# Expert halves of a mixture layer as one float32 product each, clipped straight from PSUM, with the order of all pieces drawn up anew

## What is computed

```python
h = _L0_tok_ref(x, ...)                       # gated recurrence; 257 positions come out
h = h + _L0_attn_ref(_layernorm(h), ...)      # 8 heads; k and v from a sequence of the other half of the batch
h = h + _L0_ffn_ref(_layernorm(h), ...)       # mixture of 16 experts, best 2, and a shared one

def swiglu5(h, alpha, gate_scale, up_shift, gate_clamp_raw, up_clamp_raw):
    g = jnp.clip(h[..., ::2], -gate_clamp, gate_clamp)
    u = jnp.clip(h[..., 1::2], -up_clamp, up_clamp)
    return g * jax.nn.sigmoid(g * alpha) * gate_scale * (u + up_shift)
# every expert on every position, then the weighted sum:
he = jnp.einsum('nd,edh->enh', xf, expert_w1) + expert_b1[:, None, :]
te = swiglu5(he, ...)
oe = jnp.einsum('enh,ehd->end', te, expert_w2) + expert_b2[:, None, :]
y = jnp.einsum('ne,end->nd', cw, oe)
```

## Time and profile before

| | us |
|---|---|
| median of 3 runs | 441.05 |
| lowest and highest run | 439.95 and 443.12 |
| span of the profiled execution, first to last instruction | 434.7 |
| PE, DVE busy | 334.7, 322.2 |
| ACT, POOL busy | 243.9, 157.3 |

### The profile page before, as it was taken

One profiled execution on the slowest core, in us unless ns is written; L12 is line 12 of the kernel. 1 busy time (PEld: TensorE's weight loads), 2 busy tenths in 40 slices (PEclk: granted clock), 3 DMA queues, 4 the chain that ended last, 5 costly groups with the idle time before them and its releaser, 6 DMA issues.

```text
span 434.7 us, 6229 instructions
## 1 busy us (share of the span) xinstructions
PE 334.7 (77%) x2160; PEld 269.7 (62%) x2160; DVE 322.2 (74%) x500; ACT 243.9 (56%) x412; POOL 157.3 (36%) x125
## 2 busy tenths in 40 slices
PE   4028089875787998997869998987799997778863
PEld 1015068554477685884658676967677786667752
DVE  7894577235488779696798599696884599697991
ACT  2647425543466755863666566834584685475541
POOL 1000751010054585341346466330242165163761
PEclk9658558987976999996987999998899999698995
DMA  7302900006600000029000000065000000000000
GB/s 283 155 0 99 169 1 2 2 0 171 98 0 2 0 2 2 0 99 147 24 0 0 0 0 0 0 178 90 2 0 2 2 0 2 19 8 0 1 2 24
DMA packets 12407, 17.21 MB, mean 40 GB/s; under 512 B 984, under 2 KB 9184, under 8 KB 12256
## 3 DMA queue, kind: packets, MB, share of 16 engines
q1 hardware_dynamic: 12384, 16.91, 15.9%
HBM read 11.63 MB, written 5.28 MB: 39 GB/s over the span
## 4 chain that ended last, share of the span: by engine, by line
PE 38%; DVE 36%; issue 8%; DMA 8%; ACT 4%; SPq 4%; POOL 1%; POOLq 0%; DVEq 0%; ACTq 0%
PE slot L956 37%; DVE tbuf L881 6%; DVE gbuf L869 5%; DMA ks<-spill 4%; DVE ubuf L875 4%; DVE mx L783 4%; DVE rden L798 2%; SPq L409 2%; DMA spill<-qhl 2%; DVE ubuf L891 2%; SPq L403 1%; DVE rmax L712 1%; DMA cst<-in_consts 1%; DVE zs L733 1%; DVE h2n L802 1%
## 5 line engine op out<-in xcount | busy, mean ns | idle before, releaser
L498 POOL TENSOR_TENSOR te<-tbuf,ubuf 128x516 f32<-128x516 f32 x52 | 71.6, 1378 | 70.1 <-DVE tbuf L881 52.5
L956 PE MATMUL slot<-xh,w1h 128*128 128x258 f32 x208 | 67.8, 326 | 6.9 <-DVE ubuf L891 5.0
L956 PE MATMUL slot<-te,w 128*128 128x258 f32 x208 | 53.8, 406 | 13.6 <-POOL te L498 13.6
L956 PE MATMUL slot<-xl,w1h 128*128 128x258 f32 x208 | 61.8, 297 | 0.0
L956 PE MATMUL slot<-xh,w1l 128*128 128x258 f32 x208 | 61.8, 297 | 0.0
L488 POOL TENSOR_TENSOR ubuf<-ubuf,cwb 128x516 f32<-128x516 f32 x24 | 33.7, 1403 | 76.6 <-ACT cwb L660 76.1
L956 PEld LDWEIGHTS slot<-te,w 128*128 128x128 f32 x208 | 40.0, 199 | 24.3 <-POOL te L498 18.0
L869 DVE TENSOR_SCALAR gbuf<-gbuf,fpar 128x516 f32<-128x516 f32 x52 | 48.0, 923 | 5.7 <-ACT gbuf L640 5.6
L783 DVE TENSOR_REDUCE mx<-slot 128x2 f32<-128x514 f32 x64 | 41.8, 686 | 13.0 <-PE slot L956 12.9
L956 PEld LDWEIGHTS slot<-xh,w1h 128*128 128x128 f32 x208 | 42.6, 205 | 12.2 <-DVE ubuf L891 5.6
L640 ACT ACTIVATE gbuf<-slot,cst 128x516 f32<-128x516 f32 x52 | 36.1, 694 | 19.9 <-PE slot L956 18.4
(11 more groups left out here) (161 smaller groups left out, 643.2 us busy)
## 6 DMA issues: line engine op xcount, KB each, us to landing
qs<-spill SPq DMA_DIRECT2D x12, 258.0 KB, 4.4
ks<-spill SPq DMA_DIRECT2D x24, 129.0 KB, 5.8
spill<-qhl SPq DMA_DIRECT2D x4, 516.0 KB, 2.9
spill<-khl SPq DMA_DIRECT2D x4, 516.0 KB, 3.6
...
te<-in_sel SPq DMA_DIRECT2D x1, 832.0 KB, 11.1
```

The costliest lines, as they stand in the source:

```text
L498: g.tensor_tensor(te[:, c % NTE, :, :], tbuf[:, c % NB, :, :], ubuf[:, c % NB, :, :], ALU.mult)\
L956: return nc.tensor.matmul(out_, lhsT, rhs, start=start, stop=stop, **k)
```

## The change

A half becomes one float32 product of the weights by the input, two instructions in the program (one per sequence) in place of six. The bias moves into the weights: the features of the normalised input sum to zero, so feature 0's weight row can be subtracted from all rows, which frees that row for the bias (and, for the up half, bias plus shift), with the input's feature 0 set to one. `copy` (ACT, an affine copy with a scale and a bias per partition) makes that input in place of the split by ACT and DVE. The clips of DVE now read PSUM and write gbuf and ubuf, and release the slot; the two copies by ACT per chunk are gone. Once, at the start, DVE subtracts the row and adds the shift in place of the split of the weights, and SP loads one more array of 1664 KB and a row of 6.5 KB. All of `TIMES` is new.

```diff
     "FAT": {
-        "chunk": {"g": 0.0, "clip_up_1": 0.29, "u": 0.44, "gated_1": 0.69, "cw_1": 0.67, "clip_gate": 0.47},
+        "chunk": {"g": 0.017, "clip_gate": 0.019, "u": 0.575, "clip_up": 0.622, "gated_1": 0.664, "cw_1": 0.681},
...
-            sp.dma_start(w1_stage, w1_in).then_inc(s_w1, 16)
+            sp.dma_start(w1[:, :, :, :].rearrange("p k c n -> p (k c n)"), w1_in).then_inc(s_w1, 16)
+            sp.dma_start(w0_stage, w0_in).then_inc(s_w1, 16)
+            sp.dma_start(shift_stage, shift_in).then_inc(s_w1, 16)
...
-                        act.wait_ge(s_w1, 16)
-                        a(w1h[:, :, :, :].rearrange("p k c n -> p (k c n)"), w1_stage, ACT.Copy).then_inc(s_high, 1)
...
-                a(xh[:, :, :], xn2[:, :, :], ACT.Copy).then_inc(S["xh"], 1)
+                first = const("first")
+                a(xf[:, :, :], xn2[:, :, :], ACT.Identity, bias=first[:, 1:2], scale=first[:, 0:1]).then_inc(S["xf"], 1)
...
-            def gate_half(st, u, c):
-                filled(act, st, ("g", c))
-                if c >= NB:
-                    ge(act, "gg", NF * u + c + 1 - NB)
-                release(a(gbuf[:, c % NB, :, :], slot(st, ("g", c))[:, :, 0:W], ACT.Identity, bias=par[:, B1G, c:c + 1]),
-                        st, ("g", c))
...
-            def tanh(u, c):
-                ge(act, "gclip", NF * u + c + 1)
+            def clip_gate(st, u, c):
+                released(act, st, ("g", c))
...
-            def split(st, u):
-                ge(dve, "xh", u + 1)
-                v.tensor_tensor(xl[:, :, :], xn2[:, :, :], xh[:, :, :].bitcast(F32), ALU.subtract).then_inc(S["xl"], 1)
-
             def clip_gate(st, u, c):
-                released(dve, st, ("g", c))
-                p = c % NB
-                v.tensor_scalar(gbuf[:, p, :, :], gbuf[:, p, :, :], fpar[:, GHI, c:c + 1], fpar[:, GLO, c:c + 1],
-                                ALU.min, ALU.max).then_inc(S["gclip"], 1)
+                name = ("g", c)
+                filled(dve, st, name)
+                ge(dve, "gg", NF * u + max(0, c + 1 - NB))
+                release(v.tensor_scalar(gbuf[:, c % NB, :, :], slot(st, name)[:, :, 0:W], fpar[:, GHI, c:c + 1],
+                                        fpar[:, GLO, c:c + 1], ALU.min, ALU.max), st, name)
...
-            def low_weights():
-                dve.wait_ge(s_high, 1)
-                then(v.tensor_tensor(w1l[:, :, :, :].rearrange("p k c n -> p (k c n)"), w1_stage,
-                                     w1h[:, :, :, :].rearrange("p k c n -> p (k c n)").bitcast(F32), ALU.subtract))
+            def fold_inputs():
+
+                dve.wait_ge(s_w1, 48)
+                then(v.tensor_tensor(w1[:, :, :, :].rearrange("p k c n -> p (k c n)"),
+                                     w1[:, :, :, :].rearrange("p k c n -> p (k c n)"), w0_stage, ALU.subtract))
+                up_bias = w1[0:1, 1, :, :].rearrange("p c n -> p (c n)")
+                then(v.tensor_tensor(up_bias, up_bias, shift_stage, ALU.add))
...
                 for s in range(2):
-                    o = slot(st, name)[:, s, 0:W]
-                    mm(o, w1h[:, k, c, :], xh[:, s, :], stop=False)
-                    mm(o, w1h[:, k, c, :], xl[:, s, :], start=False, stop=False)
-                    last = mm(o, w1l[:, k, c, :], xh[:, s, :], start=False)
+                    last = mm(slot(st, name)[:, s, 0:W], w1[:, k, c, :], xf[:, s, :])
                 fill(last, st, name)
```

More of the change, by code:

```diff
@@ L74 @@
     "FAT": {
-        "chunk": {"g": 0.0, "clip_up_1": 0.29, "u": 0.44, "gated_1": 0.69, "cw_1": 0.67, "clip_gate": 0.47},
[L76 to L85, removed]
+        "chunk": {"g": 0.017, "clip_gate": 0.019, "u": 0.575, "clip_up": 0.622, "gated_1": 0.664, "cw_1": 0.681},
+        "down": (5.755, 10.144, 13.709),
+        "add": (5.969, 10.326, 14.276),
+        "out": 20.644,
@@ L86 @@
+        "project": {"center": 9.925, "variance": 10.709, "scale": 11.145, "project": 11.934},
     },
     "FA": {
[L88 to L93, removed]
@@ L94 @@
-        "norm": {"center": 9.1, "variance": 10.05, "scale": 11.38, "gate": 12.1},
-        "route": (12.68, 13.66, 14.06, 14.17, 14.45),
-        "late": {"split": 15.0, "cwt": 15.1, "keep": 16.01},
+        "chunk": {"g": -0.288, "clip_gate": -0.079, "u": 0.519, "clip_up": 0.7, "gated_1": 0.051, "cw_1": 0.7},
+        "down": (6.268, 10.406, 14.138),
+        "add": (6.278, 10.413, 16.432),
+        "out": 16.957,
+        "attend": ({"begin": -0.048, "max": 0.332, "mlast": 0.2, "mtop": 0.328, "plast": 0.336, "st": 0.337, "pv": 0.0, "norm": 0.627},
+                   {"begin": 2.144, "max": 0.398, "mlast": 0.267, "mtop": 0.3, "plast": 0.294, "st": 0.136, "pv": 0.202, "norm": 2.922}),
@@ L97 @@
+        "norm": {"center": 9.134, "variance": 10.641, "scale": 11.221, "gate": 11.982},
+        "route": (12.68, 13.007, 14.04, 14.17, 15.568),
+        "late": {"copy": 13.182, "cwt": 14.662, "keep": 14.752},
     },
     "F": {
-        "chunk": {"g": 0.0, "clip_up_1": 0.11, "u": 0.4, "gated_1": 0.69, "cw_1": 0.7, "clip_gate": 0.47},
-        "down": (5.69, 10.26, 13.85),
-        "add": (6.22, 10.25, 14.63),
-        "out": 17.19,
+        "chunk": {"g": -0.497, "clip_gate": -0.223, "u": -0.25, "clip_up": -0.156, "gated_1": 0.478, "cw_1": -0.027},
@@ L103 @@
+        "down": (6.297, 10.413, 15.749),
+        "add": (6.569, 10.209, 15.785),
+        "out": 16.331,
     },
     "AT": {
-        "attend": ({"begin": -0.09, "max": 0.2, "mlast": 0.21, "mtop": 0.5, "plast": 0.33, "st": 0.36, "pv": 0.15, "norm": 0.2},
-                   {"begin": 1.65, "max": 0.4, "mlast": 0.37, "mtop": 0.33, "plast": 0.4, "st": 0.22, "pv": 0.2, "norm": 0.43}),
-        "norm": {"center": 9.1, "variance": 10.05, "scale": 11.1, "gate": 12.02},
-        "route": (12.16, 13.23, 13.66, 14.06, 14.07),
@@ L209, in use, with build @@
         return n % NSLOT, before
-def build(nc, x_in, consts_in, sel_in, w1_in, w2_in, spill, out):
+def build(nc, x_in, consts_in, sel_in, w1_in, w0_in, shift_in, w2_in, spill, out):
     ctx = ExitStack()
```

94 lines of the change are left out of this document (49 added, 45 removed).

## The result

The changed kernel takes 447.44 us (446.27 to 452.37, 4 runs) against 440.50 us (439.69 to 443.12, 4 runs) for the kernel before beside it: ratio 1.021 (95% interval 1.015 to 1.027). It is slower, by 1.5 to 2.7%.

A forecast was written before the change was run, and what follows sets the result against it. It took PE and DVE, neither full, to be bound by waiting for each other in a circle each step. Terms -1.2 - 1.8 + 0 - 4.5 = -7.5 us gave span 427.2, plus 6.35: 433.5 us, range 421 to 446.

The forecast's parts named there:

- Loop, two steps: Both loop steps: -1.9 us from h1 to q, +1.0 us from first maximum to h2n, each step; -1.8 us together.
- Rival 1: First maximum to h2n, three steps: PE waits more, at lower clock; +9.0 us a step, 446 to 457 us; chance 0.17.
- Rival 2: Whole kernel: DVE was the bound, its contention vanishes (-15 us) and PE's clock rises; 424 to 427 us; chance 0.22.
- Rival 3: Whole kernel: no difference, PE's +13.5 us eat DVE's 15 us; 440 us; chance 0.20.
- One half: PE, each of 104 halves: 0.90 us for 0.77, 0.13 us dearer, adding 13.5 us at full clock.
- One clip: DVE, each clip out of PSUM: 0.69 us, taken from L891, bounds 0.55 and 1.5; DVE busy 15 us less.
- First and second step: Before the loop: nothing in the first step; q's transfer starts earlier in the second, -1.2 us.
- h2n to the spill: Loop, h1 to q: four dearer halves replace six and the gate; -1.9 us a step.
- Spill to the next maximum: Loop, the way through memory: transfers unchanged, rest of F still the later end in the first step; 0 us.
- Step without T: Up to h2n +1.0 us, then -1.0 us with PE coming out ahead of DVE; 0 us in sum.
- Last step: Last step: DVE's clips shorten and PE becomes the bound; -4.5 us, to 53 to 54 us.
- The time: Whole kernel: span 427.2 us plus 6.35 us between span and median time gives 433.5 us.

The follow-up runs named there:

- att_direct: Kernel before with clips out of PSUM, releasing the slot, for chunks 0 to 8 in both loop steps and throughout the last step; 447.9 us, ratio 1.024.
- c_old: Kernel before with all clips reading PSUM, each right behind its product, ACT's copies gone, biases left out, three float32r products kept; 454.1 us, ratio 1.032.
- p_only: Kernel before with one float32 product a half in place of three float32r, order and ACT's copies kept; 446.2 us, ratio 1.014.
- co: Changed kernel's table and PSUM clips, but with the three float32r products of the kernel before, biases left out; 449.0 us.
- hold_old: Kernel before, ACT's copies and SBUF clips kept, but DVE's clip releases the slot and stands right behind its product; 480.0 us.
- pos_only: Kernel before with each clip placed right behind its product, ACT's copy still releasing the slot (control for hold_old); 461.9 us, ratio 1.048.
- f_clip: Kernel before with clips out of PSUM in the last step only, right behind their products, old order, bias folded into weights; 431.1 us, ratio 0.984.
- pc_old: Changed kernel with the table of the kernel before, each clip right behind the product it reads; 460.4 us, ratio 1.047.
- fa_direct: Kernel before with PSUM clips in the last step, in the changed order, and for chunks 9 to 12 of the step without T; 434.5 us, ratio 0.988.

## Why the prediction was wrong

- **The step that failed** is in "Loop, two steps": +1.0 us a step from the first maximum to h2n. It let PE's 4.0 us of extra work vanish into PE's 8.6 us of idle time but for 2.1 us, and gave DVE a gain of 1.1. Measured: PE's work grew by 4.1 and 7.4 us, its idle time did not shrink but grew by 3.5 and 0.8, and the stretches by 7.6 and 7.8 us. "A slot is now released by DVE in its own order, and PE waits for DVE where ACT had freed it" stood under ACT and had no price. In before's table, with no work added, clips that read PSUM cost +6.3 and +5.7 us in att_direct and +7.1 and +5.7 in c_old, while the product alone costs these stretches nothing (p_only). In after the table changed too, so its +7.6 and +7.8 us are not split: co, with the old product, has +10.4 and +8.1.
- **Rival 1** had the place and the size ("a loss once those stretches grow by more than 3.5 us each", 446 us in its mild form), but not the mechanism: the clock in the stretch is 0.92 and 0.90, on the whole no lower than before's 0.88 and 0.91. Of its sum the 2 us of waits were the right part (PE idles 3.5 and 0.8 us more). Rival 2's clock did rise a little (0.870 to 0.892 over the span), and its 15 us of DVE did not come. Rival 3's balance was not what happened.
- **One half.** 0.88 us to the next float32 product, 0.90 forecast, and 0.15 us more a half than three float32r products where PE is full, 0.13 forecast. PE's total came out at 347.9 us. In the old table the product costs 6 us, in the new one none that can be told (co).
- **One clip.** 0.80 us, not 0.69, so L891 was no measure of it: 104 x 0.11 = 11.4 us. `gated` went from 0.900 to 0.956 us, 2.9 us more. That is the 14 us by which DVE missed. The clip never stretches, as forecast. The Trainium skill ("VectorE: DVE Perf Modes", the errata table) has 120 cycles and one per element for a read of PSUM, by which a clip of 516 would be an estimated 0.66 us; the traces say 0.80. The same page of the Trainium skill (Rules for kernel authors) offers a choice between reading PSUM and copying out first by the number of operations; in hold_old against pos_only, who frees the slot weighs 18.1 us with the same operations.
- **First and second step.** -1.7 us for -1.2; but from the first maximum to unit 1's spill nothing was won (44.6 to 44.4 us), so the q forecast was wrong and the rest lies in the start, which varies by more among the runs (first maximum of all at 54.4 to 62.5 us).
- **h2n to the spill.** -1.7 us a step, -1.9 forecast: right.
- **Spill to the next maximum.** +1.5 and +3.1 us where nothing was forecast. In the second loop step the transfer, 5.75 us in the earlier trace rows, no longer ends last. The chain of after runs through the routing on DVE, the transposes and PE's next halves (start us, us, what):

```profile
305.62 1.34 DVE gl L810
309.46 1.33 PE slot L1071 x5
310.79 1.07 PE slot L1123 x5
311.85 1.73 PE slot L939 x4
```

  "In the first loop step the rest of F stays the later end" held for both steps.
- **Step without T.** +0.6 us in the first part (+1.0 forecast), +0.5 in the second (-1.0): with clips of 0.80 us DVE (25.69 us busy) stayed ahead of PE (23.93), so PE did not come out ahead.
- **Last step.** 51.9 us where 53.7 was forecast, PE busier than DVE as said (43.5 and 38.5 us). The clips are worth 8.6 us by themselves (f_clip), and the float32 product gives 2.7 of it back (co 49.2, after 51.9; 5.1 in the old order, c_old 49.6, pc_old 54.7).
- **The time.** The 6.35 us between span and time are 1.8 in after, so a right sum of the stretches would have given a time some 4.5 us too high.

Open: the runs do not tell whether some other order of the loop would let clips out of PSUM pay; only two tables and three placements were run. Nor do they say why four direct chunks behind copied ones cost 3.2 us (fa_direct). They do not part the 6 us a stretch of c_old and att_direct into the clip's early place and the release by DVE: pos_only has about as much by the place alone, behind a copy that c_old does not have. And hold_old holds a slot for a copy and a clip, so its 18.1 us is not the price of the release in after.
